# Attention blocks of a fused graph network on one core: roots between weight lows, a cast and two operand splits moved, the first key product in two passes

## The reference

```python
for i in range(NUM_BLOCKS):        # 4
    y = _cond_layer_norm(x, cond, s1_w[i], s1_b[i], b1_w[i], b1_b[i])
    y = _sparse_attention(y, src, dst, wq[i], bq[i], wk[i], bk[i], wv[i], bv[i], wo[i], bo[i])
    x = x + y
    y = _cond_layer_norm(x, cond, s2_w[i], s2_b[i], b2_w[i], b2_b[i])
    y = jax.nn.relu(y @ m_w1[i] + m_b1[i]) @ m_w2[i] + m_b2[i]
    x = x + y
```

## Time and profile before

| | |
|---|---|
| median of 3 runs | 851.95 us |
| profiled execution | 849.76 us, span 848.2 us |
| TensorE busy | 823.0 us, 97% of the span |
| VectorE / ScalarE / GpSimd busy | 560.2 / 395.1 / 232.8 us |
| attention blocks, about | 218 to 335, 335 to 451, 451 to 567, 567 to 684 us |
| granted TensorE clock, mean | 0.997 |

### The profile page before, as it was taken

One profiled execution on the slowest core, in us unless ns is written; L12 is line 12 of the kernel. 1 busy time (PEld: TensorE's weight loads), 2 busy tenths in 40 slices (PEclk: granted clock), 3 DMA queues, 4 the chain that ended last, 5 costly groups with the idle time before them and its releaser, 6 DMA issues.

```text
span 848.2 us, 13171 instructions
## 1 busy us (share of the span) xinstructions
PE 823.0 (97%) x4218; PEld 631.0 (74%) x4219; DVE 560.2 (66%) x1229; ACT 395.1 (47%) x646; POOL 232.8 (27%) x258
## 2 busy tenths in 40 slices
PE   5999979999899999999999999999999999999998
PEld 3666647777578788777797787887777967688786
DVE  7999998687887577477656666684767666720210
ACT  4999984444445513366223465134552244530200
POOL 4000024434512233411246022343112515422200
PEclk9999999999999999999999999999999999999999
DMA  9999965817442644653473646536436676030101
GB/s 186 202 218 226 269 159 144 198 63 177 124 122 57 185 102 143 157 114 112 96 202 101 146 88 178 125 130 153 104 118 157 186 212 181 13 100 1 49 13 38
DMA packets 59350, 113.44 MB, mean 134 GB/s; under 512 B 4372, under 2 KB 4936, under 8 KB 59292
## 3 DMA queue, kind: packets, MB, share of 16 engines
q1 hardware_dynamic: 42108, 79.00, 40.4%
q10 hardware_dynamic: 17184, 33.69, 12.1%
HBM read 105.33 MB, written 7.34 MB: 133 GB/s over the span
## 4 chain that ended last, share of the span: by engine, by line
PE 68%; DVE 2%; ACT 2%; DMA 1%; POOL 1%; issue 0%; DVEq 0%
PE ring L2030 24%; PE ring L1744 22%; PE ring L2339 5%; PE ring L1762 5%; PE mix_ps L1773 4%; PE ring L2326 3%; PE ring L2266 1%; PE ring L2267 1%; DMA wraw<-in_L_gnn_wv 1%; PE ring L2220 1%; PE ring L2221 1%; PE ring L2225 1%; PE ring L2297 1%; POOL wl L686 1%; ACT yp L988 0%
## 5 line engine op out<-in xcount | busy, mean ns | idle before, releaser
L686 POOL TENSOR_TENSOR wl<-wraw,wh 128x512 fp32r<-128x512 f32 x140 | 181.6, 1330 | 331.1 <-ACT wh L770 317.1
L695 POOL TENSOR_TENSOR rstd<-ve,half 128x1 f32<-128x1 f32 x48 | 26.4, 553 | 215.7 <-DVE ve L1173 215.4
L1846 PE MATMUL ring<-ohs,ohd 128*128 128x512 f32 x312 | 77.4, 399 | 2.8 <-DVE ohs L1345 2.8
L1846 PEld LDWEIGHTS ring<-ohs,ohd 128*128 128x128 f32 x312 | 57.4, 189 | 27.2 <-issue 14.8
L1323 DVE SCALAR_TENSOR_TENSOR ohd<-iota,dstT,vals 128x256 fp32r x156 | 69.6, 482 | 3.0 <-issue 1.8
L770 ACT ACTIVATE wh<-wraw 128x2048 fp32r<-128x2048 f32 x35 | 66.8, 1909 | 8.2 <-DMA wraw<-in_L_gnn_root 4.5
L795 ACT ACTIVATE yT_h<-ring 128x512 fp32r<-128x512 f32 x32 | 18.4, 598 | 99.4 <-PE ring L1762 99.4
L819 ACT ACTIVATE ohs<-iota,minus_srcT 128x512 fp32r<-128x512 f32 x78 | 52.2, 713 | 9.4 <-issue 6.5
L1744 PE MATMUL ring<-yT_h,wh 128*128 128x512 f32 x128 | 49.9, 390 | 1.2 <-DVE yT_l L1155 1.2
L1155 DVE TENSOR_TENSOR PT_l<-ring,PT_h 128x512 fp32r<-128x512 f32 x64 | 39.7, 682 | 16.4 <-ACT PT_h L795 16.4
L1744 PE MATMUL ring<-yT_h,wl 128*128 128x512 f32 x128 | 49.9, 389 | 0.0
(11 more groups left out here) (389 smaller groups left out, 2135.2 us busy)
## 6 DMA issues: line engine op xcount, KB each, us to landing
quad<-in_L_gnn_basis SPq DMA_DIRECT2D x60, 960.0 KB, 11.0
wraw<-in_L_gnn_m_w ACTq DMA_DIRECT2D x8, 1024.0 KB, 6.6
mix_scratch<-mixed SPq DMA_DIRECT2D x128, 32.0 KB
wraw<-in_L_gnn_wv ACTq DMA_DIRECT2D x4, 1024.0 KB, 8.5
wraw<-in_L_gnn_wq ACTq DMA_DIRECT2D x4, 1024.0 KB, 5.3
wraw<-in_L_gnn_wk ACTq DMA_DIRECT2D x4, 1024.0 KB, 5.5
wraw<-in_L_gnn_wo ACTq DMA_DIRECT2D x4, 1024.0 KB, 5.2
wraw<-mix_scratch ACTq DMA_DIRECT2D x4, 1024.0 KB, 5.6
```

Source lines behind the costliest of these rows:

```text
L686: last = g.tensor_tensor(wl[s][:, k, :], wraw[s][:, k, :], wh[s][:, k, :].bitcast(F32), ALU.subtract)
L1846: last = te.matmul(ring[:, banks[b], :], ohd[:, s, b, :], ohs[:, s, :], start=False, stop=False)
```

## The change

1. `block_lows` (GpSimd): the low of weight 6 is made in parts (piece 0, piece 1, pieces 2 and 3), each ahead of the root of rows 0, 1 and 2 of the next norm; before, all four pieces stood ahead of the first root.
2. ScalarE, blocks 2 to 4: the cast of the key weight stands behind the highs of turned rows 2 and 3, not ahead of value 1.
3. VectorE: the first block's `split_cond(1, 1)` goes from ahead of value 3 to behind the key of head 2 (head 1 of the loop). `split_cond(0, ...)`, in every block behind the scaling of head 0, goes behind the key of head 2 as well, in the first block behind the key of head 3 (head 2 of the loop).
4. TensorE: key 0 of every block is made in two passes: the eight products of the high weight, which wait only for its cast, then the four of the low weight. The wait for the low stood ahead of the whole product.

"Bias products kept" names nothing in the diff.

```diff
@@ block_lows
-                for j in (5, 6):
-                    low_weight(i * 6 + (W1 + j), j % 3)
+                low_weight(i * 6 + (W1 + 5), 5 % 3)
                 for t in range(NT):
+                    if t < 3:
+                        low_part(i * 6 + (W1 + 6), 6 % 3, ((0,), (1,), (2, 3))[t])
                     if last:
                         root_and_mean(INTO_L2 + t, t)
                     else:
@@ block_highs
                     value(0)
-                    hwi(2)
                     value(1)
                     norm_rows("a", 2)
                     norm_rows("a", 3)
+                    hwi(2)
                     value(2)
@@ attention_block, vector
                 key(0)
-                if first:
-                    split_cond(1, 1)
                 value(3)
 
                 masked(0)
                 scaled(0)
-                split_cond(0, i * 2 + 2)
                 query(1)
                 key(1)
                 for h in range(1, HEADS):
@@
                     if h + 1 < HEADS:
                         query(h + 1)
                         key(h + 1)
+                    if first and h == 1:
+                        split_cond(1, 1)
+                    elif h == (2 if first else 1):
+                        split_cond(0, i * 2 + 2)
@@ query_key, tensor
                     columns_product("q", h, wq, yT_h, yT_l)
-                    if h == 0:
-                        weight(2)
-                    columns_product("k", h, wk, yT_h, yT_l)
+                    if h:
+                        columns_product("k", h, wk, yT_h, yT_l)
+                        return
+                    out = begin(T, b, ("k", 0))
+                    pe.wait_ge(weight_hi, i * 6 + (W1 + 3))
+                    part(out, [p for k in range(KT) for p in three(cols(wk[0], k, 0), cols(wk[1], k, 0), yT_h[:, k, :], yT_l[:, k, :])[:2]], first=True)
+                    weight(2)
+                    part(out, [(cols(wk[1], k, 0), yT_h[:, k, :]) for k in range(KT)], last=True).then_inc(tile_ready, 1)
```

## The result

| | before | after |
|---|---|---|
| median, us | 851.11 (849.90 to 853.38, 4 runs) | 864.36 (858.96 to 868.17, 4 runs) |
| ratio of after to before | | 1.0148, 95% interval 1.0086 to 1.021 |
| profiled execution, us | 849.76 | 858.96 |
| its span, us | 848.2 | 857.4 |

The change makes the kernel slower by 13 us, 1.5%. The forecast for the profiled execution was 858.9 and it took 858.96; the forecast for the median was 861.0, and it is 3.4 us higher. So there are two questions: whether the 9.2 us of the profiled execution come from where the prediction put them, and where the rest of the median comes from.

The account below looks back on a forecast made before the run. TensorE, almost always busy in the blocks, was taken as the bound, so waits are paid in full. Terms -0.7 - 0.5 + 8.8 + 1.5 = +9.1 us took the profiled execution to 858.9, the median to 861.0; range 856 to 864.5.

Parts of the forecast that it names:

- old place, first block: Ahead of head 1's scores, first block: without the split TensorE's 0.58 us idle and a slow restart go, -0.7 us.
- head 1, four blocks: Fourth scores tile of head 2: split beside GpSimd's pieces makes turned lows 3.7 us late; TensorE waits 2.2 us per block.
- first block, head 2: Split behind head 3's key, GpSimd idle: VectorE 1.93 us late, slack 0.37 at the second output tile, +1.5 us.
- roots, end of the second block: Transposes of tiles 0 and 1: with one piece ahead of the first root, idle 0.30 and 0.25 us go, -0.5 us.
- key cast, two passes: Block starts: key lows end later, but the key's second pass begins 1.7 us after them; no gain, no wait.
- sum, without the clock: All terms together: +9.1 us on the profiled execution, with no drop of TensorE's granted clock counted.
- the slack of 1.58: Head 1: turned lows can be 1.58 us late before TensorE waits at the fourth scores tile of head 2.
- The precedent: One split in the trace beside four such pieces: cast 1.77 us, subtraction 2.20, GpSimd's pieces 6.92 instead of 5.05.
- The turns: VectorE's split and GpSimd's pieces alternate, a whole instruction each, at four heads; 861.0 us, chance 0.68.
- lock without turns: Rival: VectorE keeps the port pair from cast to subtraction, so head 1 costs 5.4 us, not 8.8; 857.6, chance 0.09.
- The median: Step from profiled execution to median: the kernel before's 2.2 us gap is kept, so 858.9 becomes 861.0 us.
- The clock: Rival: TensorE's granted clock drops after each of the four waits, 1.7 us a drop; 867.8 us, chance 0.05.

Follow-up runs that it names:

- the run with one more cast: Changed kernel with the cast of each conditioning split done twice, the second waiting for the first; 872.37 us, ratio 1.0252 to the kernel before.
- second measurement: The changed kernel measured once more, with nothing altered; 865.30 us (5 runs), ratio 1.0164 to the kernel before.

## Why the prediction was right, and where it was not

The direction, the place and the mechanism held. Step by step, start-to-start with the restart:

| step of the prediction | forecast, us | measured, us |
|---|---|---|
| old place, first block | -0.7 (0.58 to 0.8) | -0.77 |
| head 1, four blocks | 4 x 2.2 = +8.8 | 4 x (2.10 + 0.11) = +8.8 |
| first block, head 2 | +1.5 | 0.34 + 0.81 + 0.16, restarts 0.19, = +1.5 |
| roots, end of the second block | -0.5 | -0.46 and 0.05 = -0.5 |
| key cast, two passes | 0 | 0, covered by 1.75 |
| sum, without the clock | +9.1 | +9.0, and +9.0 and +8.9 in the table above |

- **Head 1.** The forecast lateness of 3.7 us was 3.68; the slack of 1.58 held in every kernel. Four latenesses give it: 1.92, 1.98, 3.68 and 5.34 us, less 1.58, are 0.34, 0.40, 2.10 and 3.76, and the waits were 0.34, 0.43, 2.10 and 3.78. The precedent carried over closely, 2.19 us for the subtraction and 1.53 for the cast where it had 2.20 and 1.77; that the cast waits less was foreseen. GpSimd's four pieces took 6.43, not near 7: in the precedent a third VectorE instruction stood beside them (a subtraction at 179.58, 1.65 us), which the prediction does not mention. The turns themselves are shown by the run with one more cast.
- **The lock.** The pieces and the split stretch each other, and neither does when they are apart; between two VectorE instructions GpSimd gets a whole piece in. The rival "lock without turns", 857.6, is out. The Trainium skill's page "SBUF — State Buffer", section "SBUF: two separate sides", has the shared pair of ports as an exclusive lock for a whole instruction; the runs agree with it.
- **Old place.** From the transposes ahead of it to the first scores product of head 1 TensorE took 2.49 us before and 1.72 after. The restart that the prediction added is no gain: this product takes 0.50 us after the change too, where nothing is waited for. The bounds 0.58 to 0.8 were too narrow: against 1.72 the loss was 0.70 to 1.33 us in the five profiled executions that had the split in the old place. A wait that is measured once has a spread of its own; one execution gave the point, not the ends.
- **First block, head 2.** The size held, the place only in part. The prediction priced the second output tile, which lost 0.16 of the 1.5 us; most was lost at the first, and 0.34 at the fourth scores tile of head 3, where its own slack of 1.58 gives just that. The sum is right since a tile waits only for what the tiles before it have not yet waited for: in all about the lateness of 1.93 less the smallest slack, 0.37.
- **Roots and key.** Both terms held, the roots' partly by luck: the 0.30 us of idle time was 0.46 from start to start, and the 0.25 at tile 1 was hardly a wait for a root, as 0.20 of it stayed. That a late key weight no longer reaches TensorE was not seen in any run.
- **The median.** This is the one step that failed: "The median of the three runs is 2.2 us above it, at 851.95; I set the sum on that." It takes the clock of the changed kernel to be that of the old one. The rival "The clock" had the right mechanism and the right price (1.7 us for a drop) and got a chance of 0.05 on one piece of evidence: no fall after a wait of 0.58 us. That was evidence about short waits, and the change makes waits of 2.1. What came lies between the two: one to three falls in the blocks of the three profiled executions with four such waits, not none and not four. The profiled execution had one in the blocks and none ahead of them, where that of the kernel before had one; that is why its forecast came out to 0.1 us, partly by luck.

The range (856 to 864.5) held the median with 0.1 us to spare, and that was luck: its second measurement gave 865.30, outside, and so would the median of all nine runs.

## What to carry to other kernels

Before an instruction is moved, look at the queue of its own engine for the idle stretch that fits it, and at what the engine's neighbours do in that stretch: here the right place (a hole of 1.97 us ahead of a key's low) lay one step ahead of the chosen one and turned 13 us of loss into some 1 us of gain. Price a moved pair of VectorE instructions beside a run of GpSimd's by the stretched durations that the trace already has, and compare the lateness with the slack of whoever waits, here by how many tiles later the ring is reused. And where a change puts waits of some microseconds in front of a TensorE that was busy throughout, count a possible fall of its clock behind each as a case of its own.

## What the runs showed of the hardware

- VectorE's cast (0.69 us alone) and subtraction (1.28 us) beside GpSimd's queued pieces each took 0.8 to 1.1 us longer, every time, whether one, two or three stood in a row. By the times of the pieces, what is waited for is the rest of the running one; the stretch was always less than the piece's 1.28 us. VectorE's lows that read a tile of the ring stood beside the same pieces and were not stretched.
- An instruction that has begun is not stretched by one that comes later: 1.28 us for the subtraction during which GpSimd's first piece arrived.
- After a wait of 2.1 us in an otherwise busy TensorE the granted clock fell to 0.50 for 3.4 us in 8 of 14 cases, after 0.4 us in none of six, after 1.18 us in none of 13. What decides between the 8 and the 6 was not tried. Stretches at 0.50 of 3.4 or 6.8 us between 95 and 147 us, ahead of the blocks, come and go between the profiled executions, 0 to 10.2 us in all. The runs of the kernel before scatter from 847.7 to 854.5 us, and much of it goes with their mean granted clock.
